# A fused attention and feed-forward layer: who applies the norms, in which order the first loads, roots and splits go, and the first projections in passes

## The chip, the cores and the metric

One core of one Trainium2 chip. The metric is the device time of one execution in microseconds; lower is better. The engines are PE (TensorE), DVE (VectorE), ACT (ScalarE), POOL (GpSimd) and SP (SyncE, which issues every DMA of this kernel).

## The reference

Everything is float32. `x` is (4, 256, 256): four sequences of 256 tokens with 256 features.

```python
xn = _layernorm(x, axis=-1)
s = attn(xn, Wqkv, Wproj, bproj)      # 16 heads of 16; softmax over the 256 keys of each sequence
g = silu(ffn(xn))                      # gelu(xn @ proj1.T + b1) @ proj2.T + b2, hidden 1024
x = x + s * g
```

## The kernel before

To keep float32 accuracy in fast matmuls, each factor of a product is split into a high part in the fp32r type and the remainder, a low part, in the same type (names ending in h and l). A product is three products: high x high, low weight x high x, high weight x low x. The function `product` issues them as passes `(a, b)`, where a is 0 for the high and 1 for the low part of the left factor (the weights, in the projections), and b the same for the right factor, each over two chunks `kc` of the 256 features. It puts a wait ahead of the first instruction that needs a part.

One list, `build_order()`, holds all steps in PE's order. Each engine walks through the list and does its own share of each step, so the list sets the order on PE, ACT and DVE alike. POOL and SP have programs of their own. Engines meet at counting semaphores.

The head of the kernel, which the change is about:

- SP loads x by sequences of 256 tokens (256 KB each, `x_in[b]`), and the weights `wqkv` in three chunks c of 256 KB: c = 0 is the queries' weights, 1 the keys', 2 the values'. Then come w1 and w2 (1 MB each), biases and wp.
- Norm of sequence b: DVE takes the statistics (`norm_stats`, two tiles of 128 tokens) and mean, variance + eps (`norm_eps`); POOL takes the power -1/2 (`rsqrt`, `rstd`). The norm is applied in place in `xs`. For sequences 0 and 1 ACT does it as scale x + shift (L380), for which DVE first makes `shift` = -mean x rstd (L476). For sequences 2 and 3 DVE does it itself, (x - mean) x rstd (L492).
- The weights: ACT copies chunk c to `wqh` (L375, "split"), POOL subtracts and makes `wql` (L332). Likewise w1 (ACT L406, POOL L344) and w2.
- `("XT", b)`: PE transposes the normed sequence b (L657, four f32 transposes); ACT copies two chunks to `xTh` (L392), DVE makes `xTl` (L517).
- `("QA", i)`: PE multiplies weight block i (0 and 1 queries, 2 and 3 keys) with sequence 0, six matmuls of 256 columns. `("QK", 0, i)` does the same block with sequence 1 in the other half of the same bank; then ACT copies the 512 columns to `stage` (L400), DVE makes the low half of it (L528), and SP issues three DMAs that rearrange them by heads into `qs` and `ks` (L293). `("QK", 1, i)` is sequences 2 and 3. `("V", h, p)` are the values, `("F1", n)` the first layer of the feed-forward part.
- The first scores `("S", 0)` (L699) wait for the twelve DMAs of half 0 (`stacked[0]`).
- Before all this PE runs `WARM` = 6 matmuls of 128x256 f32 on zeros (L635, each is two records), and one more, `KEEP` (L661), between XT 0 and QA 0.

The PSUM banks of later steps are given out in turn (`banks()`): V 0 takes the bank of QK (0, 0), so it waits until DVE has made its low half; V 1 takes that of QK (0, 1), QK (1, 0) that of QK (0, 2).

The order begins:

```python
order = [("XT", 0), ("KEEP",), ("QA", 0), ("QA", 1), ("XT", 1), ("QA", 2), ("QA", 3)]
order += [("QK", 0, i) for i in range(4)]
order += [("XT", 2), ("V", 0, 0), ("XT", 3), ("V", 0, 1)] + [("QK", 1, i) for i in range(4)]
order += [("F1", n) for n in range(FC)]
```

Of the kernel before, what the change touches and what calls it, by code (L numbers as in the profile page):

```python
# [5 lines left out]
B, SQ, E = 4, 256, 256  # L6
NH, HN = 16, 16
F = 1024
P = 128
# [8 lines left out]
GROUPS = B * 4  # L18
STK = 48
STM = STK + 2  # L20
WARM = 6
AHEAD = 6
VW = HN + 1
PAIRS = [(j, b) for half in range(2) for j in range(HP // 2) for b in (2 * half, 2 * half + 1)]
# [2 lines left out]
def build_order():  # L27

    order = [("XT", 0), ("KEEP",), ("QA", 0), ("QA", 1), ("XT", 1), ("QA", 2), ("QA", 3)]
    order += [("QK", 0, i) for i in range(4)]
    order += [("XT", 2), ("V", 0, 0), ("XT", 3), ("V", 0, 1)] + [("QK", 1, i) for i in range(4)]
    order += [("F1", n) for n in range(FC)]
    order += [("V", 1, p) for p in range(2)]

    ffn = [("F2", u, part) for u in range(TT) for part in range(4)]  # L40
    filler = [(s, 1) for s in ffn[:4 * TT // 2]] + [(("F1", n), 1.9) for n in range(FC, 2 * FC)]
    filler += [(s, 1) for s in ffn[4 * TT // 2:4 * TT // 2 + AHEAD]]
    ffn = ffn[4 * TT // 2 + AHEAD:]
    share = sum(w for _, w in filler) / len(PAIRS)
    at = 0
    for n in range(len(PAIRS)):
        while filler and at < (n + 1) * share - 0.5:
            step, w = filler.pop(0)
            order.append(step)
            at += w  # L50

        order += [("S", 2 * n), ("S", 2 * n + 1)]
        if n >= 2 and PAIRS[n - 2][1] == B - 1 and PAIRS[n - 2][0] < 2:
            order.append(("MT", PAIRS[n - 2][0]))
    assert not filler

    order.append(ffn.pop(0))
    for g in range(GROUPS):
        j, b = divmod(g, B)
        order += [("ST", 2 * g), ("ST", 2 * g + 1)]  # L60
        if g >= 1:
            order.append(("PV", g - 1))

        if g >= 1 and (j == 0 or b <= 1):
            order.append(ffn.pop(0))
        if g in (1, 2):
            order.append(("MT", g + 1))
        if g == GROUPS - 2:
            order.append(("GATE",))
        if b == 3:  # L70
            order.append(("TURN", 0, j))
        if b == 1 and j >= 1:
            order.append(("TURN", 1, j - 1))
        if b >= 2 and j >= 1:
            u = 2 * (j - 1) + b - 2
            if g < GROUPS - 1:
                order += [("PJ", u, 0), ("PJ", u, 1), ("FIN", u)]
            else:

                order += [("PJ", u, 0), ("PV", g), ("PJ", u, 1)]  # L80
    assert not ffn
    return order + [("PJ", 6, 0), ("PJ", 7, 0), ("TURN", 1, 3), ("FIN", 5), ("PJ", 6, 1), ("FIN", 6),
                    ("PJ", 7, 1), ("FIN", 7)]


def layer_kernel(nc, x, wqkv, w1, b1, w2, b2, wp, bp, out):
    f32, f32r = mybir.dt.float32, mybir.dt.float32r
    ALU, ACT, AX = mybir.AluOpType, mybir.ActivationFunctionType, mybir.AxisListType
    order = build_order()
# [5 lines left out]
    with ctx:  # L95
        def sem(name):
            return ctx.enter_context(nc.semaphore(name))
# [7 lines left out]
        def at(name, shape, dtype, where=None):  # L105
            size = 4
            for n in shape[1:]:
                size *= n
            if where is None:
                where = used[0]  # L110
                used[0] += (size + 31) // 32 * 32
                assert used[0] <= slab * 4, (name, used[0])
            return nc.alloc_sbuf_tensor_at(name, shape, dtype, offset=base + where)
# [53 lines left out]
        veps = at("veps", [P, TT], f32)  # L167
        mhalf = at("mhalf", [P, TT], f32)
        rstd = at("rstd", [P, TT], f32)
        shift = at("shift", [P, 4], f32)  # L170
        negm = at("negm", [P, HP // 2, 2, 2, 2, B], f32)
        mm = at("mm", [2 * HP * 2, 2, 2, P], f32r)
        rc = at("rc", [P, 2, SQ // 32], f32)
# [13 lines left out]
            sem(n) for n in ("wqkv_hi", "wqkv_lo", "w1_hi", "w1_lo", "w2_hi", "w2_lo"))  # L187
        stats_done, mv_done, veps_done, rstd_done, xn_done = (
            sem(n) for n in ("stats_done", "mv_done", "veps_done", "rstd_done", "xn_done"))
        shift_done = sem("shift_done")  # L190
        xt_made, xt_hi, xt_lo = sem("xt_made"), sem("xt_hi"), sem("xt_lo")
        qk_made, qk_hi, qk_lo = sem("qk_made"), sem("qk_hi"), sem("qk_lo")
        v_made, v_out, f1_made, gelu_done = sem("v_made"), sem("v_out"), sem("f1_made"), sem("gelu_done")
# [65 lines left out]
        def _(sp):  # L259
# [2 lines left out]
            out_t = out.rearrange("(b p t) e -> p b t e", p=P, t=2)  # L262
            for b in range(2):
                sp.dma_start(xs[:, 2 * b:2 * b + 2, :], x_t[:, b, :]).then_inc(x_in[b], 16)
            for c in range(2):
                sp.dma_start(wqkv_raw[:, c], wqkv[c]).then_inc(wqkv_in[c], 16)
            for b in range(2, B):
                sp.dma_start(xs[:, 2 * b:2 * b + 2, :], x_t[:, b, :]).then_inc(x_in[b], 16)
            sp.dma_start(wqkv_raw[:, 2], wqkv[2]).then_inc(wqkv_in[2], 16)
# [45 lines left out]
        def _(pool):  # L315
# [8 lines left out]
            def rsqrt(b):  # L324
                pool.wait_ge(veps_done, b + 1)
                nc.gpsimd.tensor_tensor(rstd[:, 2 * b:2 * b + 2], veps[:, 2 * b:2 * b + 2],
                                        mhalf[:, 2 * b:2 * b + 2], ALU.pow).then_inc(rstd_done, 1)

            pool.wait_ge(mhalf_set, 1)
            def low_wqkv(c):  # L330
                pool.wait_ge(wqkv_hi, c + 1)
                nc.gpsimd.tensor_tensor(wql[:, c], wqkv_raw[:, c], wqh[:, c].bitcast(f32),  # L332
                                        ALU.subtract).then_inc(wqkv_lo, 1)

            rsqrt(0)
            low_wqkv(0)
            rsqrt(1)
            low_wqkv(1)
            rsqrt(2)
            rsqrt(3)  # L340
            low_wqkv(2)
            for kc in range(KC):
                pool.wait_ge(w1_hi, kc + 1)
                nc.gpsimd.tensor_tensor(w1l[:, kc, :], w1_raw[:, kc, :], w1h[:, kc, :].bitcast(f32),  # L344
# [24 lines left out]
        def _(act):  # L369
# [4 lines left out]
                act.wait_ge(wqkv_in[c], 16)  # L374
                nc.scalar.activation(wqh[:, c], wqkv_raw[:, c], ACT.Copy).then_inc(wqkv_hi, 1)  # L375

            def norm_apply(b):
                act.wait_ge(shift_done, b + 1)
                for t in (2 * b, 2 * b + 1):
                    nc.scalar.activation(xs[:, t, :], xs[:, t, :], ACT.Identity, scale=rstd[:, t:t + 1],  # L380
                                         bias=shift[:, t:t + 1]).then_inc(xn_done, 1)

            split_wqkv(0)
            norm_apply(0)
            split_wqkv(1)
            n_qk = n_v = n_f1 = n_mt = 0
            for s in order:
                if s[0] == "XT":
                    b = s[1]
                    act.wait_ge(xt_made, b + 1)  # L390
                    for kc in range(KC):
                        nc.scalar.activation(xTh[:, kc, b * SQ:(b + 1) * SQ], bank[:, home[("XT", b)][kc], 0:SQ],  # L392
                                             ACT.Copy).then_inc(xt_hi, 1)
                    if b == 0:
                        norm_apply(1)
                        split_wqkv(2)
                elif s[0] == "QK":
                    h, i = s[1:]
                    act.wait_ge(qk_made, n_qk + 1)
# [66 lines left out]
        def _(dve):  # L466
# [3 lines left out]
                for t in (2 * b, 2 * b + 1):  # L470
                    nc.vector.bn_stats(stats[:, t, :], xs[:, t, :]).then_inc(stats_done, 1)

            def norm_shift(b):

                dve.wait_ge(rstd_done, b + 1)
                nc.vector.scalar_tensor_tensor(shift[:, 2 * b:2 * b + 2], mv[:, 2 * b:2 * b + 2, 0], -1.0,  # L476
                                               rstd[:, 2 * b:2 * b + 2], ALU.mult, ALU.mult).then_inc(shift_done, 1)

            def norm_eps(b):

                for t in (2 * b, 2 * b + 1):
# [20 lines left out]
            nc.vector.memset(warm[:], 0.0).then_inc(warm_set, 1)  # L502
            norm_stats(0)
            norm_eps(0)
            norm_stats(1)
            norm_shift(0)
            norm_eps(1)
            norm_stats(2)
            norm_shift(1)
            n_qk = n_mt = 0  # L510
            for s in order:
                if s[0] == "XT":
                    b = s[1]
                    cols = slice(b * SQ, (b + 1) * SQ)
                    for kc in range(KC):
                        dve.wait_ge(xt_hi, KC * b + kc + 1)
                        nc.vector.tensor_tensor(xTl[:, kc, cols], bank[:, home[("XT", b)][kc], 0:SQ],  # L517
                                                xTh[:, kc, cols].bitcast(f32), ALU.subtract).then_inc(xt_lo, 1)
                    if b == 0:
                        norm_eps(2)  # L520
                        norm_stats(3)
                    if b == 1:
                        norm_eps(3)
                        norm_apply(2)
                elif s[0] == "QK":
                    h, i = s[1:]
                    dve.wait_ge(qk_hi, n_qk + 1)
# [81 lines left out]
        def _(pe):  # L609
            def product(dst, lhs, rhs, chunks, first=True, last=True, rhs_hi=None, lhs_lo=None, rhs_lo=None,  # L610
                        passes=((0, 0), (1, 0), (0, 1))):

                todo = [(kc, a, b) for a, b in passes for kc in chunks]
                for n, (kc, a, b) in enumerate(todo):
                    if rhs_hi and (a, b) == (0, 0):
                        pe.wait_ge(rhs_hi[0], rhs_hi[1] + n + 1)
                    if rhs_lo and (a, b) == (0, 1):  # L620
                        pe.wait_ge(rhs_lo[0], rhs_lo[1] + n - 2 * len(chunks) + 1)
                    if lhs_lo and (a, b, kc) == (1, 0, chunks[0]):
                        pe.wait_ge(*lhs_lo)
                    m = nc.tensor.matmul(dst, lhs(kc, a), rhs(kc, b), start=first and n == 0,  # L624
                                         stop=last and n == len(todo) - 1)
                return m
# [7 lines left out]
                for _ in range(WARM):  # L634
                    nc.tensor.matmul(bank[:, 7, 0:HALF // 2], warm[:, 0:P], warm[:], start=True, stop=True)  # L635

            def project(s, at, width):

                i = s[2]
                cols = slice(at, at + width)  # L640
                seen = KC * (cols.stop // SQ - 1)
                return product(bank_of(*s)[:, at % HALF:at % HALF + width],
                               lambda kc, a: (wqh, wql)[a][:, i // 2, kc, (i % 2) * P:(i % 2 + 1) * P],
                               lambda kc, a: (xTh, xTl)[a][:, kc, cols], range(KC),
                               rhs_hi=(xt_hi, seen), lhs_lo=(wqkv_lo, i // 2 + 1), rhs_lo=(xt_lo, seen))

            pe.wait_ge(warm_set, 1)
            warm_up()
# [1 line left out]
            for s in order:  # L650
# [10 lines left out]
                    nc.tensor.matmul(bank[:, 7, 0:P], warm[:, 0:P], warm[:, 0:P], start=True, stop=True)  # L661
                elif s[0] == "QA":
                    pe.wait_ge(wqkv_hi, s[1] // 2 + 1)
                    project(("QK", 0, s[1]), 0, SQ)
                elif s[0] == "QK":
                    h, i = s[1:]
                    pe.wait_ge(wqkv_hi, i // 2 + 1)
# [133 lines left out]
```

## Time and profile before

| | us |
|---|---|
| median of 3 runs | 134.61 |
| lowest and highest | 133.0, 134.88 |
| the profiled execution, its own time | 134.43 |
| its span in the trace | 132.6 |

The span is what the trace covers, from the first to the last instruction of that execution; the 1.8 us beside it are start and end, outside the trace. All rows below are of this one execution. PEclk is the share of TensorE's full speed that was granted, 1.00 for 2.4 GHz and 0.50 for 1.2 GHz. In a timeline an xN row joins N instructions that follow one another; its second number is from the start of the first to the end of the last, so that instructions 0.12 us apart and 0.28 long show as x2 with 0.40.

### The profile page before, as it was taken

The page shows a single profiled execution, that of the slowest core. Times are in us where ns is not written, and L with a number is a line of the kernel's source. Part 1 is how long each engine was busy: PE and PEld are TensorE (multiplying, and loading weights), DVE is VectorE, ACT ScalarE, POOL GpSimd, SP SyncE. Part 2 cuts the span into 40 slices and gives each one's busy share as a digit, 9 for nine tenths or more (in the row PEclk, how much of TensorE's full clock was granted, in tenths as well). Part 3 has the DMA queues.
Part 4 walks back from the last instruction along what each step waited for, and adds up shares of the span by engine and source line. Part 5 has one row for each costly group of instructions (what it writes and reads, how often), then busy time and mean ns, then how long its engine had stood idle before and what let it go on. Part 6 is the DMA issues. An engine that isn't in the chain of part 4 may idle for free.

```text
span 132.6 us, 2665 instructions
## 1 busy us (share of the span) xinstructions
PE 123.1 (93%) x1002; PEld 94.8 (72%) x1002; DVE 88.0 (66%) x176; ACT 77.2 (58%) x119; POOL 51.2 (39%) x53
## 2 busy tenths in 40 slices
PE   6959999999999999999998999699999999999960
PEld 5639999888899989887676697466665666576550
DVE  0664584440001999999996899566768666858983
ACT  4264497489992101117658505769869787987610
POOL 3292468039999100005656560069604000004400
PEclk9995999999999999999999999999999999999995
DMA  4999459999999999940000000800000110110103
GB/s 134 325 400 395 115 121 146 159 164 141 166 167 147 168 169 147 168 66 7 0 0 0 2 12 10 302 14 10 15 0 5 40 42 5 40 42 2 42 2 119
DMA packets 7553, 13.29 MB, mean 100 GB/s; under 512 B 1012, under 2 KB 2676, under 8 KB 7284
## 3 DMA queue, kind: packets, MB, share of 16 engines
q1 hardware_dynamic: 7540, 13.11, 46.8%
q8 instruction: 8, 0.13, 0.5%
q14 instruction: 5, 0.04, 0.1%
HBM read 5.51 MB, written 1.05 MB: 49 GB/s over the span
## 4 chain that ended last, share of the span: by engine, by line
PE 74%; DVE 8%; ACT 6%; issue 4%; DMA 3%; POOL 1%; SPq 1%; ACTq 0%; DVEq 0%
PE bank L624 49%; PE bank L747 11%; PE bank L719 7%; PE bank L699 6%; DMA wqkv_raw<-wqkv 3%; ACT PT L450 3%; DVE negm L540 3%; PE bank L657 1%; DVE cd L557 1%; ACT hG L432 1%; POOL wql L332 1%; ACT cTh L462 1%; DVE shift L476 1%; DVE yh L582 1%; DVE fin L599 1%
## 5 line engine op out<-in xcount | busy, mean ns | idle before, releaser
L540 DVE TENSOR_REDUCE negm<-bank 128x4 f32<-128x1024 f32 x32 | 37.1, 1218 | 16.1 <-PE bank L699 16.0
L450 ACT ACTIVATE PT<-bank 128x1024 f32<-128x1024 f32 x32 | 30.7, 1020 | 6.4 <-PE bank L719 6.3
L353 POOL TENSOR_TENSOR hTl<-hG,hTh 128x512 fp32r<-128x512 f32 x16 | 20.4, 1293 | 23.3 <-ACT hTh L436 23.3
L363 POOL TENSOR_TENSOR bg<-gate,bps 128x256 f32<-128x256 f32 x8 | 6.1, 765 | 33.8 <-DVE gate L499 24.8
L747 PE MATMUL bank<-PT,VA 128*17 128x256 f32 x256 | 16.9, 382 | 0.0
L456 ACT ACTIVATE th<-yh 128x256 f32<-128x256 f32 x8 | 3.3, 418 | 21.4 <-DVE yh L582 21.4
L624 PE MATMUL bank<-w2h,hTh 128*128 128x256 f32 x64 | 14.7, 311 | 0.5 <-DVE yh L582 0.3
L719 PE MATMUL bank<-qs,ks 50*128 50x256 f32 x128 | 12.9, 310 | 1.4 <-ACT PT L450 1.4
L557 DVE STREAM_TRANSPOSE cd<-bank 128x256 f32<-128x256 f32 x16 | 7.2, 449 | 10.3 <-PE bank L747 10.3
L432 ACT ACTIVATE hG<-bank,b1s 128x512 f32<-128x512 f32 x16 | 10.9, 679 | 5.1 <-PE bank L624 5.1
L624 PEld LDWEIGHTS bank<-w2h,hTh 128*128 128x128 f32 x64 | 9.7, 189 | 5.5 <-issue 4.6
L624 PE MATMUL bank<-w2h,hTl 128*128 128x256 f32 x64 | 12.8, 282 | 0.0
L624 PE MATMUL bank<-w2l,hTh 128*128 128x256 f32 x64 | 12.8, 282 | 0.0
L719 PEld LDWEIGHTS bank<-qs,ks 50*128 50x128 f32 x128 | 8.8, 185 | 4.5 <-ACT PT L450 2.2
L699 PE MATMUL bank<-ks,qs 48*128 48x256 f32 x128 | 11.8, 303 | 0.0
L699 PEld LDWEIGHTS bank<-ks,qs 48*128 48x128 f32 x128 | 8.5, 185 | 3.5 <-issue 1.8
L624 PE MATMUL bank<-xTh,w1h 128*128 128x512 f32 x32 | 10.5, 410 | 0.4 <-ACT hG L432 0.4
L436 ACT ACTIVATE hTh<-hG 128x512 fp32r<-128x512 f32 x16 | 10.1, 633 | 0.5
L624 PEld LDWEIGHTS bank<-w2l,hTh 128*128 128x128 f32 x64 | 9.9, 191 | 0.0
L624 PE MATMUL bank<-xTh,w1l 128*128 128x512 f32 x32 | 9.9, 390 | 0.0
L624 PE MATMUL bank<-xTl,w1h 128*128 128x512 f32 x32 | 9.9, 390 | 0.0
L624 PEld LDWEIGHTS bank<-w2h,hTl 128*128 128x128 f32 x64 | 9.9, 190 | 0.0
(76 smaller groups left out, 212.0 us busy)
## 6 DMA issues: line engine op xcount, KB each, us to landing
qs<-stage SPq DMA_DIRECT2D x12, 256.0 KB, 13.1
ks<-stage SPq DMA_DIRECT2D x12, 256.0 KB, 18.7
w_raw<-w SPq DMA_DIRECT2D x2, 1024.0 KB, 8.2
xs<-x SPq DMA_DIRECT2D x4, 256.0 KB, 3.8
xb<-x SPq DMA_DIRECT2D x1, 1024.0 KB, 5.4
out<-fin SPq DMA_DIRECT2D x8, 128.0 KB, 1.7
wqkv_raw<-wqkv SPq DMA_DIRECT2D x3, 256.0 KB, 4.5
wps<-wp SPq DMA_DIRECT2D x8, 32.0 KB, 6.5
```

Of the source, the lines that this page charges most:

```text
L353: nc.gpsimd.tensor_tensor(hTl[:, n % FC, :], hG[:, n % FC, :], hTh[:, n % FC, :].bitcast(f32), ALU.subtract).then_inc(h_lo, 1)
L363: nc.gpsimd.tensor_tensor(bg[:, u % 2, :], gate[:, u, :], bps[:], ALU.mult).then_inc(bg_done, 1)
L432: nc.scalar.activation(hG[:, f, :], bank_of(*s), ACT.Gelu, bias=b1s[:, f:f + 1]).then_inc(gelu_done, 1)
L436: nc.scalar.activation(hTh[:, f, :], hG[:, f, :], ACT.Copy).then_inc(h_hi, 1)
L450: nc.scalar.activation(PT[:, w % 4], scores_of(*s), ACT.Exp).then_inc(exp_done, 1)
L456: nc.scalar.activation(th[:, u % 2, :], yh[:, u % 2, :], ACT.Tanh).then_inc(th_done, 1)
L540: nc.vector.tensor_reduce(negm[:, j, :, :, s[1] % 2, b].rearrange("p q a -> p a q"), scores_of(*s), axis=AX.X, op=ALU.max, negate=True).th ...
L557: nc.vector.transpose(cd[:, g % 2, :], bank_of(*s)[:, 0:SQ]).then_inc(cd_out, 1)
L624: m = nc.tensor.matmul(dst, lhs(kc, a), rhs(kc, b), start=first and n == 0, stop=last and n == len(todo) - 1)
L699: last = nc.tensor.matmul(scores_of(*s)[:, par, qt, :], qs[rows, hp, c:c + P], ks[rows, hp, b * SQ:(b + 1) * SQ], start=True, stop=True)
L719: last = nc.tensor.matmul(scores_of(*s)[:, par, kt, :], ks[rows, hp, c:c + P], qs[rows, hp, b * SQ:(b + 1) * SQ], start=True, stop=True)
L747: last = nc.tensor.matmul(bank_of(*s)[32 * m:32 * m + VW, 0:SQ], VA[:, 2 * b + kt, 4 * j + m, :], PT[:, w % 4, m % 2, kt, :], start=(kt == ...
```

## The change

1. SP loads x 0, weights 0, x 1, weights 1, x 2, x 3, weights 2, in place of x 0, x 1, weights 0, weights 1, x 2, x 3, weights 2.
2. DVE applies the norm of all four sequences. `shift` is gone, and ACT applies none.
3. DVE's order: stats 0, eps 0, apply 0, stats 1, eps 1; after the low part of XT b, for b = 0 and 1: apply b+1, stats b+2, eps b+2. Apply 3 stays behind the low half of the first QK.
4. ACT splits weight chunk 1 behind its copies of XT 0 and chunk 2 behind those of XT 1.
5. POOL's root of sequence c goes ahead of the low part of weight chunk c for c = 0, 1, 2, and the root of sequence 3 goes behind the low part of chunk 2 (before, it went ahead of it).
6. The projections of sequence 0 go in passes: for the query blocks 0 and 1 high x high of both, low weights of both, low x of both; for the key blocks high x high and low x of both, then XT 1, then the low weights of both. XT 1 moves behind these passes. The waits in `product` count by chunk.
7. `WARM` is 4 in place of 6.

```diff
-WARM = 6
+WARM = 4
...
-    order = [("XT", 0), ("KEEP",), ("QA", 0), ("QA", 1), ("XT", 1), ("QA", 2), ("QA", 3)]
+    order = [("XT", 0), ("KEEP",)]
+    order += [("QA", i, a, b) for a, b in ((0, 0), (1, 0), (0, 1)) for i in (0, 1)]
+    order += [("QA", i, a, b) for a, b in ((0, 0), (0, 1)) for i in (2, 3)]
+    order += [("XT", 1)] + [("QA", i, 1, 0) for i in (2, 3)]
...
             for b in range(2):
                 sp.dma_start(xs[:, 2 * b:2 * b + 2, :], x_t[:, b, :]).then_inc(x_in[b], 16)
-            for c in range(2):
-                sp.dma_start(wqkv_raw[:, c], wqkv[c]).then_inc(wqkv_in[c], 16)
+                sp.dma_start(wqkv_raw[:, b], wqkv[b]).then_inc(wqkv_in[b], 16)
...
-            def low_wqkv(c):
+            for c in range(3):
+                rsqrt(c)
                 pool.wait_ge(wqkv_hi, c + 1)
                 nc.gpsimd.tensor_tensor(wql[:, c], wqkv_raw[:, c], wqh[:, c].bitcast(f32),
                                         ALU.subtract).then_inc(wqkv_lo, 1)
-
-            rsqrt(0)
-            low_wqkv(0)
-            rsqrt(1)
-            low_wqkv(1)
-            rsqrt(2)
             rsqrt(3)
-            low_wqkv(2)
...
             split_wqkv(0)
-            norm_apply(0)
-            split_wqkv(1)
...
-                    if b == 0:
-                        norm_apply(1)
-                        split_wqkv(2)
+                    if b <= 1:
+                        split_wqkv(b + 1)
...
             norm_stats(0)
             norm_eps(0)
+            norm_apply(0)
             norm_stats(1)
-            norm_shift(0)
             norm_eps(1)
-            norm_stats(2)
-            norm_shift(1)
...
-                    if b == 0:
-                        norm_eps(2)
-                        norm_stats(3)
-                    if b == 1:
-                        norm_eps(3)
-                        norm_apply(2)
+                    if b <= 1:
+                        norm_apply(b + 1)
+                        norm_stats(b + 2)
+                        norm_eps(b + 2)
...
-                        pe.wait_ge(rhs_hi[0], rhs_hi[1] + n + 1)
+                        pe.wait_ge(rhs_hi[0], rhs_hi[1] + kc + 1)
...
-                        pe.wait_ge(rhs_lo[0], rhs_lo[1] + n - 2 * len(chunks) + 1)
+                        pe.wait_ge(rhs_lo[0], rhs_lo[1] + kc + 1)
...
-                    project(("QK", 0, s[1]), 0, SQ)
+                    end = (1, 0) if s[1] >= 2 else (0, 1)
+                    project(("QK", 0, s[1]), 0, SQ, passes=(s[2:],), first=s[2:] == (0, 0), last=s[2:] == end)
```

## Rows read from the trace of the kernel before

**Rows 1.** The page, busy time of PE: us (share of the span) and instructions.
```profile
PE 123.1 (93%) x1002; PEld 94.8 (72%) x1002; DVE 88.0 (66%) x176; ACT 77.2 (58%) x119; POOL 51.2 (39%) x53
```

**Rows 2.** The chain of waits in order of time: start us, us, what.
```profile
1.65 4.28 DMA wqkv_raw<-wqkv
...
5.95 0.64 ACT wqh L375
...
10.22 2.19 PE bank L624 x8
...
13.27 4.53 PE bank L624 x36
```

**Rows 3.** Stretches: PE, PEld, DVE, ACT, POOL busy (instructions), PEclk, DMA share, GB/s.
```profile
6.70:10.20 3.50, 1.86 (x10) 1.27 (x10) 2.34 (x5) 2.37 (x6) 3.12 (x3) 1.00 1.02 407
10.20:13.60 3.40, 3.38 (x15) 3.34 (x16) 1.27 (x6) 1.57 (x5) 0.69 (x1) 0.50 1.01 390
13.70:70.00 56.30, 56.30 (x383) 48.46 (x383) 36.36 (x51) 29.80 (x51) 27.53 (x19) 1.00 0.78 118
```

**Rows 4.** Timeline: start us, us, engine, line, what, count [idle before <-releaser].
```profile
1.19 5.49 PE L635 MATMUL bank<-warm 128*128 128x256 f32 x12 [1.19 <-DVE warm L502]
...
3.45 0.75 DVE L471 BATCH_NORM_STATS2 stats<-xs 128x6 f32<-128x256 f32 x2 [2.32 <-DMA xs<-x]
...
4.78 0.71 POOL L326 TENSOR_TENSOR rstd<-veps,mhalf 128x2 f32<-128x2 f32 x1 [2.76 <-DVE veps L485]
...
6.48 1.08 ACT L380 ACTIVATE xs<-xs,shift,rstd 128x256 f32<-128x256 f32 x2
...
7.21 0.84 PE L657 MATMUL bank<-ident,xs 128*128 128x128 f32 x4 [0.54 <-ACT xs L380]
...
8.08 0.66 ACT L392 ACTIVATE xTh<-bank 128x256 fp32r<-128x256 f32 x2
...
8.54 1.28 POOL L332 TENSOR_TENSOR wql<-wqkv_raw,wqh 128x512 fp32r<-128x512 f32 x1
...
8.61 0.57 PE L624 MATMUL bank<-xTh,wqh 128*128 128x256 f32 x2 [0.34 <-ACT xTh L392]
8.61 1.22 DVE L476 SCALAR_TENSOR_TENSOR shift<-mv,rstd 128x2 f32<-128x2 f32 x1 [0.58 <-POOL rstd L326]
...
10.22 0.92 PE L624 MATMUL bank<-xTl,wqh 128*128 128x256 f32 x2 [0.81 <-DVE xTl L517]
...
12.21 1.05 PE L657 MATMUL bank<-ident,xs 128*128 128x128 f32 x4
...
13.30 0.66 ACT L392 ACTIVATE xTh<-bank 128x256 fp32r<-128x256 f32 x2 [1.83 <-PE bank L657]
...
15.67 1.32 ACT L400 ACTIVATE stage<-bank 128x512 fp32r<-128x512 f32 x2 [1.71 <-PE bank L624]
...
16.30 0.69 DVE L528 SCALAR_TENSOR_TENSOR stage<-bank,stage 128x512 fp32r<-128x512 f32 x1 [0.83 <-ACT stage L400]
...
17.09 3.91 SPq L293 DMA_DIRECT2D qs<-stage  x6
...
17.64 0.60 PE L657 MATMUL bank<-ident,xs 128*128 128x128 f32 x4
...
42.12 0.74 PE L699 MATMUL bank<-ks,qs 48*128 48x256 f32 x8
```

**Rows 5.** Single lines of the code: duration ns min/median/max, first and last start us.
```profile
L380 ACT ACTIVATE xs<-xs,shift,rstd x4: 585/585/600, 6.5 to 10.4; 128x256 f32<-128x256 f32 x4
L492 DVE TENSOR_SCALAR xs<-xs,mv,rstd x4: 404/408/409, 14.7 to 17.2; 128x256 f32<-128x256 f32 x4
L536 DVE TENSOR_SCALAR b2s<-b2s x1: 284/284/284, 28.3 to 28.3; 128x256 f32<-128x256 f32 x1
```

**Rows 6.** Landing of the second DMA (x 1), and of ks copies issued 23.0 to 25.0.
```profile
DMA to landing us min/median/max: 2.8/2.8/2.8
...
DMA to landing us min/median/max: 12.2/14.0/15.1
```

More of the change, by code:

```diff
@@ L169, in layer_kernel @@
         rstd = at("rstd", [P, TT], f32)
-        shift = at("shift", [P, 4], f32)
         negm = at("negm", [P, HP // 2, 2, 2, 2, B], f32)
@@ L189, in layer_kernel @@
             sem(n) for n in ("stats_done", "mv_done", "veps_done", "rstd_done", "xn_done"))
-        shift_done = sem("shift_done")
         xt_made, xt_hi, xt_lo = sem("xt_made"), sem("xt_hi"), sem("xt_lo")
@@ L375, in split_wqkv @@
                 nc.scalar.activation(wqh[:, c], wqkv_raw[:, c], ACT.Copy).then_inc(wqkv_hi, 1)
[L377 to L381, printed above, removed]
             split_wqkv(0)
-            norm_apply(0)
-            split_wqkv(1)
             n_qk = n_v = n_f1 = n_mt = 0
@@ L471, in norm_stats @@
                     nc.vector.bn_stats(stats[:, t, :], xs[:, t, :]).then_inc(stats_done, 1)
[L473 to L477, printed above, removed]
             def norm_eps(b):
@@ L635, in warm_up, with project @@
                     nc.tensor.matmul(bank[:, 7, 0:HALF // 2], warm[:, 0:P], warm[:], start=True, stop=True)
-            def project(s, at, width):
+            def project(s, at, width, **passes):
                 i = s[2]
@@ L644, in project @@
                                lambda kc, a: (xTh, xTl)[a][:, kc, cols], range(KC),
-                               rhs_hi=(xt_hi, seen), lhs_lo=(wqkv_lo, i // 2 + 1), rhs_lo=(xt_lo, seen))
+                               rhs_hi=(xt_hi, seen), lhs_lo=(wqkv_lo, i // 2 + 1), rhs_lo=(xt_lo, seen), **passes)
             pe.wait_ge(warm_set, 1)
```

## The prediction

> **What bounds the kernel now.** I read first the busy shares and the granted clock of the page: PE is busy 93% of the span [rows 1], and no other engine above 66%. An edit to the head is worth time only if the matmuls behind it start earlier, so I went to the chain of waits [rows 2]. The reader is to see in it two parts. Up to 10.2 us it hops between engines: the load of the first weights, their split on ACT, then their low part and a root on POOL, a norm's shift on DVE, the low half of x. From 10.22 us it is PE without a break, of which two pieces stand in the rows. From 13.7 to 70 us PE is busy for all of 56.30 us [rows 3], and the other engines are started by its products there. So what the change is worth is by how much the dense stretch gets ahead. I measure this at one place: the start of the transposes of sequence 2, XT 2, now 17.64 [rows 4]. Behind it PE issues the same instructions in the same order in both kernels.
>
> Then the clock. The head has a low stretch: 0.50 granted from 10.2 to 13.6, 1.00 before and after [rows 3]. Prices differ by it. Four f32 transposes of 128 columns took 1.05 us inside (12.21) and 0.60 outside (17.64) [rows 4]; less the length of the last, 0.42 and 0.27, they are 0.21 and 0.11 apart. Projections of 256 f32r columns: 36 in 4.53 us, 0.12 to 0.13 each, nearly all outside [rows 2]; inside I take 0.21, half that speed. The 12 warm-up records took 5.49 us, 0.43 apart, for 256 f32 columns [rows 4]; from 0.11 for 128 such columns they would be 0.22 apart at the high level. So the warm-up ran at 1.2 GHz, although the clock reads 1.00 there: the rows show no level before the first switch, and by the projections at 8.61 (two in 0.57 us, against 0.92 for two at 10.22) 2.4 GHz had been reached.
>
> **Part by part.** *Norm 0 on DVE.* Now: rstd of POOL at 4.78 + 0.71 = 5.49; shift on DVE; the two applies on ACT only from 6.48, 0.59 long [rows 5], since they are queued behind the split of the weights, whose load lands at 1.65 + 4.28 = 5.93 [rows 2, 4]. XT 0 starts at 7.21. After: DVE applies from 5.53, two 0.33 us apart, as the two statistics of the same size at 3.45 (0.75 less 0.41) [rows 4], and 0.41 long [rows 5], done at 5.94 and 6.26. ACT's two norms (1.08 us the pair) and two shifts go away. XT 0, which starts 0.14 us behind the first apply (7.21 against 6.48 + 0.59), starts at 6.08. At the low level XT 1 shows 13.30 - 12.21 = 1.09 from the first transpose to the first copy on ACT [rows 4], so xTh(0) is copied from 7.17 and the first projection starts 0.53 behind (8.61 - 8.08), at 7.70 instead of 8.61. Gain here: 0.9.
>
> *Loads by turns.* The first weights move from third to second place, x of sequence 1 from second to third. The second place, issued at 1.2, landed 2.8 later at 4.0, and the third at 5.93 [rows 2, 6]. If place decides, the split is done long before 7.2; if the tensor decides, it is as now, 5.95 + 0.64 = 6.59, which also is in time, and POOL's low part is done at 7.9, in time for the second pass. x 1 at 5.93 is wanted by DVE at 6.27, behind the applies. So: nothing, and 0.3 us if x 1 came 0.7 late. The later loads keep their places.
>
> *WARM 6 to 4, and the passes.* Four warm-ups end at 1.19 + 8 x 0.43 = 4.6; none of this lies on the path, and its only price is the clock. Passes let four high matmuls run while the low weights and the low half of x are made, where now PE waits 0.81 us for xTl(0) at 10.22 with all blocks behind it [rows 4]. At the low level the 12 matmuls of the two query blocks take 12 x 0.213 = 2.56, to 10.26. The low half of x: from the start of stats 0 to that of the root went 4.78 - 3.45 = 1.33 us [rows 4], so DVE does stats 1 and eps 1 from 6.27 to 7.5, then xTl(0) (twice 0.37) to 8.25; its pass comes at 9.4, so no wait.
>
> *Norm 1.* POOL's root follows eps 1: 7.6 to 8.3; the apply follows xTl(0) on DVE: 8.34 to 9.1. Now this shift of two elements a partition takes 1.22 us [rows 4], from the start of POOL's wql(1) at 8.54 to its end at 9.82: DVE stood for POOL. The apply reads one tensor where the shift read two, and I cost it at its own 0.41. XT 1 now waits for the norms, and xTh(1) until 13.30. After: with the high level from 10.26, eight matmuls of the key blocks 10.26 to 11.25, XT 1 to 11.7, the four low-weight ones to 12.2 (POOL's low 1 is done by 9.6), xTh(1) from 11.95, QK 0 from 12.45, 24 matmuls of 0.12 = 2.9: XT 2 at 15.35. **Gain 17.64 - 15.35 = 2.3 us.**
>
> *What is late next.* DVE gets new work: the queue behind xTl(1) (12.35 to 13.05) is apply 2, stats 3, eps 3 (to 14.95), then the low half of QK 0 (0.69 [rows 4]) to 15.6, apply 3 to 16.4, QK 1 to 17.05. Waiting for these: V 0 for the first bank and POOL's wql(2) (14.5), at 15.8, just covered; XT 3 at 17.25 for apply 3, covered by 0.8; V 1 for the second bank at 17.7, covered. On POOL rstd 3 now stands behind wql(2), 1.28 us: 15.0 to 15.7, which is the time above. On ACT the splits of chunks 1 and 2 move behind the xTh copies of sequences 0 and 1, but stage 0 starts at 13.25 against 15.67 [rows 4], 2.4 earlier, so ACT's queue keeps up with PE. SP waits for the low half: its first copy of the stage leaves at 15.7 instead of 17.09, only 1.4 earlier, while PE is 2.3 earlier. The last of the 12 copies that the first S needs is issued at 25.0 and lands 15.1 later, at 40.1 [rows 6]; S starts at 42.12 [rows 4]. Slack falls from 2.0 to 1.1. It stays covered; if the copies shifted not at all, 0.3 would be lost.
>
> All of 2.3 us should arrive at the end: 134.43 - 2.3 = **132.1 us** (span 130.3). The profiled run lies 0.18 below the median, so the reference is good for either; of three runs one was at 133.0.
>
> **The rule that speaks against it.** The apply with pointer scalars takes 404 to 409 ns, a scaling by a constant of the same shape 284 [rows 5]: the apply does not run in whatever form makes the other fast. The Trainium skill (SBUF — State Buffer, Who interferes with whom) says that tensor_scalar can enter a mode that takes the pair of ports that DVE shares with GpSimd, and that the second of the two to start is then held for the whole instruction of the first. By this rule the applies would stand as the shift did; the duration speaks against it, and no row here has an apply beside a long POOL instruction.
>
> **Rivals.**
> (a) *The clock rises earlier*, before 8.6 as it did in this run, in spite of the shorter warm-up. Then the projections run at 0.12, bounded by xTl(0) at 8.25, xn(1) at 9.1 and wql(1) at 9.6: XT 1 at 9.9, QK 0 at 11.0, XT 2 at 13.9. 3.7 earlier: 130.7. For it: nothing else is in the way. Against it: PE is idle between 4.6 and 6.1 and has small work until 7.7, and with as small work from 6.7 to 10.2 (1.86 of 3.50 us busy) the level fell [rows 3].
> (b) *The clock stays low longer*, until 13.7: of the 3.4 us after 10.26 half is lost, 1.7; gain 0.6: 133.8. My 10.26 is a choice: the one low stretch shown was 3.4 us long with matmuls throughout, and I laid the same length behind the start of steady work, which is between 7.0 (XT 0's end) and 7.7, so 10.3 to 11.1. Gaps in the passes, for xTh(0), wqh(1) or the norm of sequence 1, could put the rise off.
> (c) *DVE stands for POOL after all.* Apply 3 and POOL's first w1l (twice the size of wql, so 2 x 1.28 = 2.6 us) become ready together at 15.7. If they exclude each other and POOL is first, apply 3 ends at 19.0 instead of 16.4 and XT 3 waits 1.75 us: gain 0.55, 133.9. The shift at 8.61 shows such a wait [rows 4]. Against it the duration above.
> (d) *Slower: the clock never settles in the head.* The mechanism is the cut of the warm-up from 5.5 to 3.4 us ahead of an idle 1.5; each 3.4 us at low inside dense work costs 1.7. If it also stayed low from 13.7 to 17.1, this is another 1.7: 135.5. It decides from where the low level lasts past 14.9 (gain used up: 2.3 = half of 4.6).
>
> **How the numbers follow.** Main case (rise near 10.3, the queues cover) 55%, 131.5 to 132.9: DVE's and ACT's queues are within 0.3 us of binding at two places, and an earlier or later rise by 1 us gives 0.5 either way. (a) 18%, (b) 12%, (c) 6%, (d) 4%; the last 5% something unseen, both ways. The prediction is 132.1. The range reaches from (a) to beyond (b) and (c): 130.6 to 134.1. About 2% is what a measurement here tells from no change; that border is 131.9, inside the main case, just under its middle. Faster by over 2%: all of (a), two in five of the main case and a bit: 0.43. Same: 0.52. Slower: 0.05.
>
> **What would show it.** First transposes near 6.1, first projection near 7.7; XT 1 near 11.2; XT 2 near 15.3 and PE without idle from there to the first S near 39.8; the shift's 1.22 us gone and all eight applies at 0.41; first stage copy issued near 15.7. PE's granted clock is the number to look at first: if the rise isn't at 10 to 11, (a), (b) or (d) holds, and the time follows by half of what is left at low. Wrong otherwise: a wait of V 0 for the low half of QK 0, of XT 3 for apply 3, or of S for the copies.

## The result and the profile after

The changed kernel is slower: 139.8 us median of 4 runs (139.22 to 140.82) against 134.75 of 4 (133.0 to 137.3); ratio 1.047, 95% interval 1.040 to 1.054. I had forecast 132.1, range 130.6 to 134.1. The profiled execution took 140.17 us, its span is 138.3 (before: 132.6).

Executions of one and the same kernel spread by 1 to 6% here (before: 133.0 to 137.3), so ratios below are of those within 1.5% of their kernel's fastest.

The page after, PE and granted clock in 40 slices of 3.46 us:

```profile
PE   6489955999999999999999899969999999999970
...
PEclk9968996589999999999999999999999999999999
```

PE has a hole in the sixth and seventh slice (17 to 24 us) that was not there, and the clock two dips (0.50 from 8.1 to 11.5 us and from 21.7 to 28.5), of which the second was not there. The timeline after, in the form of [rows 4]:

```profile
4.17 0.63 ACT L371 ACTIVATE wqh<-wqkv_raw 128x512 fp32r<-128x512 f32 x1 [1.94 <-DMA wqkv_raw<-wqkv]
...
5.60 1.26 POOL L335 TENSOR_TENSOR wql<-wqkv_raw,wqh 128x512 fp32r<-128x512 f32 x1
5.68 1.66 DVE L473 TENSOR_SCALAR xs<-xs,mv,rstd 128x256 f32<-128x256 f32 x2 [0.90 <-POOL rstd L328]
...
7.16 0.67 PE L634 MATMUL bank<-ident,xs 128*128 128x128 f32 x4 [2.29 <-DVE xs L473]
...
9.16 1.28 POOL L335 TENSOR_TENSOR wql<-wqkv_raw,wqh 128x512 fp32r<-128x512 f32 x1
9.23 1.68 DVE L473 TENSOR_SCALAR xs<-xs,mv,rstd 128x256 f32<-128x256 f32 x2 [0.15 <-POOL rstd L328]
...
16.48 0.60 PE L634 MATMUL bank<-ident,xs 128*128 128x128 f32 x4
...
16.65 0.68 DVE L505 SCALAR_TENSOR_TENSOR stage<-bank,stage 128x512 fp32r<-128x512 f32 x1
...
17.43 7.43 SPq L295 DMA_DIRECT2D qs<-stage  x6
17.48 4.73 POOL L340 TENSOR_TENSOR w1l<-w_raw,w1h 128x1024 fp32r<-128x1024 f32 x2
17.48 0.47 PE L601 MATMUL bank<-wqh,xTh 128*128 128x256 f32 x2 [0.41 <-DVE stage L505]
17.55 4.81 DVE L473 TENSOR_SCALAR xs<-xs,mv,rstd 128x256 f32<-128x256 f32 x2 [0.21 <-POOL rstd L328]
...
20.16 0.41 PE L634 MATMUL bank<-ident,xs 128*128 128x128 f32 x2 [1.02 <-DVE xs L473]
...
22.41 0.69 PE L634 MATMUL bank<-ident,xs 128*128 128x128 f32 x2 [1.85 <-DVE xs L473]
```

Look at DVE's applies (L473) and at the POOL row beside each. In the kernel before, a pair of applies took 0.73 us (0.41 each, 0.33 apart):

```profile
14.74 0.73 DVE L492 TENSOR_SCALAR xs<-xs,mv,rstd 128x256 f32<-128x256 f32 x2
```

Here it takes 1.66 and 1.68 beside a wql and 4.81 beside both w1l. The last pair of the change taken apart, DVE and POOL:

```profile
17.48 2.38 POOL L340 TENSOR_TENSOR w1l<-w_raw,w1h 128x1024 fp32r<-128x1024 f32 x1
17.55 2.46 DVE L473 TENSOR_SCALAR xs<-xs,mv,rstd 128x256 f32<-128x256 f32 x1 [0.21 <-POOL rstd L328]
...
19.82 2.38 POOL L340 TENSOR_TENSOR w1l<-w_raw,w1h 128x1024 fp32r<-128x1024 f32 x1
...
19.93 2.43 DVE L473 TENSOR_SCALAR xs<-xs,mv,rstd 128x256 f32<-128x256 f32 x1
```

Each apply ends 0.15 us behind the end of a POOL subtraction, and the second meets the second subtraction. XT 3 waits for both tiles: 1.02 + 1.85 us of idle PE. Then the clock, in stretches as in [rows 3]:

```profile
8.50:11.70 3.20, 3.20 (x16) 3.20 (x17) 3.05 (x8) 0.55 (x2) 1.93 (x2) 0.54 1.01 421
21.90:25.20 3.30, 2.78 (x12) 2.41 (x13) 3.30 (x8) 0.66 (x2) 0.31 (x1) 0.50 0.75 127
25.40:28.40 3.00, 3.00 (x10) 2.42 (x10) 0.08 (x1) 0.61 (x1) 0.00 (x0) 0.50 1.09 138
29.00:75.00 46.00, 46.00 (x307) 38.57 (x306) 29.15 (x33) 22.88 (x38) 19.96 (x15) 1.00 0.80 104
```

PE was nearly idle from 19.1 to 22.4 (busy 0.45 us), and the clock is at 1.2 GHz (0.50 granted) from 21.7 to 28.5. PE is busy for 6.1 us of that, so by my estimate half of this is lost, some 3.0 us.

Where the time came, by five places of PE's program (us from the start of the trace). The first three kernels are before, after, and the experiment e2, in which POOL stays out of the applies' way; e7 and e12 are the change taken apart:

| | XT 0 | XT 2 | QK (1, 0) | first S | span |
|---|---|---|---|---|---|
| before | 7.21 | 17.64 | 21.38 | 42.12 | 132.6 |
| after | 7.16 | 16.48 | 25.81 | 47.86 | 138.3 |
| e2 | 5.87 | 15.20 | 19.00 | 39.91 | 130.9 |
| e7, loads, passes, WARM alone | 7.85 | 17.16 | 20.90 | 41.69 | 132.5 |
| e12, norms, splits, roots alone | 6.16 | 15.38 | 23.53 | 45.57 | 136.5 |

Up to XT 2 the change gains 1.16 us. Between XT 2 and QK (1, 0) it loses 9.33 - 3.74 = 5.6: 0.41 for QK 0's low half, 2.9 for the applies, and 2.3 more, of which the slow clock is some 1.7 (3.4 us busy at 0.50) and the rest isn't told apart. From there to the first S another 1.3 go to the slow clock. The end is 5.7 late, as the first S is.

### The profile page after: what moved, and what is told of

Read it like the earlier page. It is cut to its first block, busy times and chain, and to the rows that moved or that the text cites. A ratio compares the mean times of both kernels' runs of the same rounds, so it can differ in the third digit from the quotient of the medians.

```text
span 138.3 us, 2663 instructions
## 1 busy us (share of the span) xinstructions
PE 124.5 (90%) x998; PEld 95.6 (69%) x998; DVE 94.8 (69%) x178; ACT 75.3 (54%) x115; POOL 51.0 (37%) x53
## 4 chain that ended last, share of the span: by engine, by line
PE 70%; DVE 15%; ACT 6%; issue 4%; DMA 2%; POOL 1%; ACTq 0%; DVEq 0%; POOLq 0%
PE bank L601 46%; PE bank L725 10%; PE bank L697 6%; PE bank L677 6%; DVE xs L473 6%; ACT PT L437 3%; DVE negm L517 3%; DMA xs<-x 2%; PE bank L634 1%; POOL rstd L328 1%; DVE stats L458 1%; DVE cd L534 1%; ACT hG L419 1%; ACT cTh L449 1%; DVE yh L559 1%
## 5 line engine op out<-in xcount | busy, mean ns | idle before, releaser
L473 DVE TENSOR_SCALAR xs<-xs,mv,rstd 128x256 f32<-128x256 f32 x8 | 9.9, 1272 | 1.3 <-POOL rstd L328 1.3
```

The costliest lines, as they stand in the source:

```text
L473: nc.vector.tensor_scalar(xs[:, t, :], xs[:, t, :], mv[:, t, 0:1], rstd[:, t:t + 1], ALU.subtract, ALU.mult).then_inc(xn_done, 1)
```

## The experiments

**e1: w1l behind apply 3.**

```diff
                 pool.wait_ge(w1_hi, kc + 1)
+                pool.wait_ge(xn_done, TT)
```

> POOL's two w1l subtractions wait until DVE has applied norm 3. Exclusion theory (an apply and a POOL subtraction can't run together; apply 3 waited for both w1l and that is the loss): apply 3 falls from 4.81 us to 0.73, XT 3 starts near 19.0 instead of 22.4, no second low stretch of the clock at 21.9, QK (1, 0) near 20.9 against 21.3 before: about 134.0 us, level with before or 0.5 below. Rival (the order of the passes, the serial queue on DVE or the shorter warm-up are the loss): stays at 138 or more.

Four runs took 134.21 to 138.63 us (before in the same set: 133.53 to 137.51). The traced one took 136.3, with this head: apply 3 took 0.73 us, XT 3 began at 19.14, there was no second low stretch at 22 (the next is at 86.9 to 90.3), QK (1, 0) came at 21.01. The exclusion theory holds for the largest piece. What I hadn't expected: the first S waited.

```profile
17.70 0.73 DVE L474 TENSOR_SCALAR xs<-xs,mv,rstd 128x256 f32<-128x256 f32 x2 [0.21 <-POOL rstd L328]
...
42.59 0.74 PE L678 MATMUL bank<-ks,qs 48*128 48x256 f32 x8 [0.76 <-DMA ks<-stage]
```

**e2: all of POOL's lows behind the applies.** As e1, and for each weight chunk

```diff
                 rsqrt(c)
                 pool.wait_ge(wqkv_hi, c + 1)
+                pool.wait_ge(xn_done, 2 * (c + 1))
```

> Besides w1l, each wql(c) on POOL waits until DVE has applied norm c. Exclusion theory: all eight applies take 0.41, XT 0 starts near 6.2 instead of 7.2, XT 2 near 15.5 instead of 16.5, QK (1, 0) near 19.2 to 19.6: 132.2 to 133.0 us, what my prediction had. Rival (POOL's later lows become the wait: V 0 for wql(2)): 134 or more.

Four runs took 132.55, 132.68, 135.05 and 136.75 us. The timeline of the one of 132.68:

```profile
5.31 0.73 DVE L475 TENSOR_SCALAR xs<-xs,mv,rstd 128x256 f32<-128x256 f32 x2 [0.91 <-POOL rstd L328]
5.87 1.09 PE L636 MATMUL bank<-ident,xs 128*128 128x128 f32 x4 [0.90 <-DVE xs L475]
...
15.20 0.60 PE L636 MATMUL bank<-ident,xs 128*128 128x128 f32 x4
...
15.57 4.62 SPq L295 DMA_DIRECT2D qs<-stage  x6
...
39.91 0.74 PE L679 MATMUL bank<-ks,qs 48*128 48x256 f32 x8
```

All pairs are back at 0.73 us, and the head is the one that I had forecast for the change itself (XT 2 at 15.35, first copy at 15.7, first S at 39.8). One hold is left, on the small eps step (0.17 us alone), which meets wql(2):

```profile
13.56 1.30 POOL L336 TENSOR_TENSOR wql<-wqkv_raw,wqh 128x512 fp32r<-128x512 f32 x1 [2.32 <-DVE xs L475]
...
14.33 0.55 DVE L468 TENSOR_SCALAR veps<-mv 128x2 f32<-128x2 f32 x1
```

It stands ahead of the low half of QK 0 in DVE's queue, so SP's first copy could leave some 0.4 us earlier still, by estimate.

**e3: the applies in a form that also accumulates.** POOL is as in the change. The accumulating form uses its second operation to reduce, so the norm's scaling is left out here.

```diff
                     nc.vector.tensor_scalar(xs[:, t, :], xs[:, t, :], mv[:, t, 0:1], rstd[:, t:t + 1],
-                                            ALU.subtract, ALU.mult).then_inc(xn_done, 1)
+                                            ALU.subtract, ALU.mult,
+                                            accum_out=spare[:, t:t + 1]).then_inc(xn_done, 1)
```

> The applies also write an accumulator that nobody reads; POOL is left as in the changed kernel. If it is the two-port form of the apply that excludes POOL, and this form has none, the applies take about 0.54 us each (twice 0.13 for 256 elements more) beside POOL's work and the time is 132.5 to 133.5. If the two pointer scalars are what is read through the shared port, the applies still wait for POOL and the time stays at 139 to 140.

Half right. The applies wait for nobody, with w1l beside them:

```profile
14.69 0.54 DVE L474 TENSOR_SCALAR_CACHE_REDUCE xs<-xs,mv,rstd 128x256 f32<-128x256 f32 x1 [0.21 <-POOL rstd L329]
14.69 4.76 POOL L341 TENSOR_TENSOR w1l<-w_raw,w1h 128x1024 fp32r<-128x1024 f32 x2
...
41.85 0.74 PE L679 MATMUL bank<-ks,qs 48*128 48x256 f32 x8 [2.94 <-DMA ks<-stage]
```

It still reads both pointer scalars, so these are not what collides. But the time is 136.57 (ratio 1.017, 1.006 to 1.029), although QK (1, 0) is at 18.05, 3.3 us ahead of before. The first S waits 2.94 us for the last copy of half 0, and the clock is at 0.50 from 42.8 to 46.2 and again from 87.1 to 90.5. The head can be made faster than the copies behind it.

**e4: WARM = 6** in the changed kernel.

> Changed kernel with WARM = 6. Exclusion theory: apply 3 still takes 4.8 us, the time stays within 0.8 us of 139.8. Clock theory (the two warm-ups that were cut are the loss): the low stretch at 8.5 to 11.7 moves or goes and the time falls by 2 us or more.

138.79 us, ratio to before 1.033 (1.022 to 1.044): 1.0 below the changed kernel in medians, more than I gave it. Apply 3 still took 4.81. In its trace there is no low stretch in the first 21 us, XT 2 is at 15.10, and the one behind the hole lasts 3.4 us where the changed kernel's lasted 6.8; there is one more, from 90.0 to 93.4. So the warm-up may be worth a microsecond here, by where the clock's switches fall; one trace of each can't settle that. It is not the loss.

**e5: SP holds its copies of half 1.** As e2, and

```diff
             for h in range(2):
+                if h == 1:
+                    sp.wait_ge(stacked[0], 192)
```

> As e2, and SP holds its copies of half 1 until the twelve of half 0 have landed. In e1 and in the accumulator run the first S waited 0.8 and 2.9 us for the last copy of half 0, which had been on its way 17.4 us, where before it was 15.1. If the copies of half 1, which now come early, slow those of half 0, the last ks copy of half 0 lands 1 us or more earlier than in e2 and no wait is left ahead of the first S; time as e2 or up to 1 us less. If the copies don't disturb one another, nothing changes. If holding them is too much, the first S of the second half (near 61) waits and the time is above e2.

The theory that the halves disturb each other isn't borne out. From the first issue to the first S: 24.7 us here, with nothing of half 1 in the queue, 24.3 in e2, and 25.8 in e13, the same kernel as e2. With such a spread between two traces of one kernel, an effect of a microsecond could hide. What the hold did was to make the second half late, by 3.67 us, with the clock at 0.50 from 62.5 to 69.3. Four runs took 136.46 to 140.37 us.

```profile
38.94 0.74 PE L681 MATMUL bank<-ks,qs 48*128 48x256 f32 x8 [0.39 <-DMA ks<-stage]
...
63.74 1.23 PE L681 MATMUL bank<-ks,qs 48*128 48x256 f32 x8 [3.67 <-DMA ks<-stage]
```

**e7: the kernel before with the loads, the passes and WARM = 4 alone.** (The diff of the change, its parts 1, 6 and 7.)

> The kernel before with the order of loads, the passes of the projections and WARM = 4 alone; norms 0 and 1 stay on ACT, POOL keeps its order. If the norms on DVE are the whole loss and the passes are worth what PE waited at 10.2 (0.8 us), this runs 0.5 to 1 us below before, XT 2 near 17. Rival (the passes or the short warm-up lose by themselves, by putting XT 1 later and by a longer low stretch): 135 to 137 us, XT 2 at 18 or later.

Neither: ratio 1.003 (0.998 to 1.007), no difference; the median of the ten runs is 134.7 us, against 134.53 of before. XT 2 came at 17.16, 0.5 earlier, in spite of an XT 0 that was 0.6 later:

```profile
6.93 0.14 DVE L478 SCALAR_TENSOR_TENSOR shift<-mv,rstd 128x2 f32<-128x2 f32 x1
7.11 1.09 ACT L382 ACTIVATE xs<-xs,shift,rstd 128x256 f32<-128x256 f32 x2 [2.27 <-DVE shift L478]
```

The shift stood behind stats 1 on DVE, and x 1 was now the third load. Passes and loads are worth something, about 0.5 us at QK (1, 0), and don't lose by themselves. Here too apply 3, which was on DVE before the change already, met wql(2): its pair took 1.25 us, covered.

**e12: norms, splits and roots alone**: the changed kernel with the loads, the order of projections and WARM of before.

> Changed kernel with the loads, the order of the projections and WARM = 6 of before: only the norms on DVE, the splits' places and POOL's order stay. Exclusion theory: apply 3 still meets w1l and the pairs of 0 to 2 meet wql, so the loss is all here: 138.5 to 140.5 us, and with the passes alone at 134.7 the two parts add up to the whole. Rival (it takes both parts for the loss): under 137.

138.82 us, ratio 1.035 (1.026 to 1.044); apply 3 again 4.81 us beside w1l, a low stretch from 22.9 to 26.3. With e7's 0.3% this is most of the 4.7%; 1 us is left.

The two parts are not independent, though. With the weights third again, wql(0) begins at 6.95 us, behind apply 0, which is free:

```profile
5.60 0.74 DVE L471 TENSOR_SCALAR xs<-xs,mv,rstd 128x256 f32<-128x256 f32 x2 [0.91 <-POOL rstd L326]
...
6.95 1.27 POOL L333 TENSOR_TENSOR wql<-wqkv_raw,wqh 128x512 fp32r<-128x512 f32 x1 [1.39 <-ACT wqh L369]
```

In the change the weights land second, wql(0) begins at 5.60 and holds the pair to 1.66 us, and XT 0 is 1.0 later (7.16 against 6.16). So the earlier weights, harmless in e7, took away the gain of norm 0. Whether this is the 1 us that is left isn't shown: e4, with the early weights but WARM = 6 as in e12, also took 138.8 us. e12 and e4 have in common that no low stretch is recorded before 21 us (XT 2 at 15.38 and 15.10), where the change has one from 8.1 to 11.5.

**e8 and e9: what form the apply has.** e8 puts constants in place of the pointers, so the norm is left out; e9 cuts each apply in two.

```diff
# e8
-                    nc.vector.tensor_scalar(xs[:, t, :], xs[:, t, :], mv[:, t, 0:1], rstd[:, t:t + 1],
+                    nc.vector.tensor_scalar(xs[:, t, :], xs[:, t, :], 0.0, 1.0,
# e9
+                    for part in range(2):
+                        half = slice(part * P, (part + 1) * P)
+                        last = nc.vector.tensor_scalar(xs[:, t, half], xs[:, t, half], mv[:, t, 0:1],
```

> Changed kernel whose applies take the constants 0.0 and 1.0 in place of mean and rstd, so the norm is left out. If the two-port form is what excludes POOL, these also wait for w1l (4.8 us for the last pair), and one alone takes 0.28 us as L536 did. If the pointer scalars are what collides, they take 0.28 us everywhere and never wait.

> Each apply of 256 columns is made as two of 128. It shows which form the apply with pointer scalars has when alone: at one column a cycle (0.13 us for 128) a half takes 0.27 us; at two, 0.34 us, and then the 0.12 us over the form with constants are a fixed cost of the pointers and say nothing of the form. My prediction took the 0.40 against 0.28 for the slow form.

The first pair of e8, its last pair, and the first of e9 (duration ns min/median/max):

```profile
L473 DVE TENSOR_SCALAR xs<-xs x2: 280/812/1345, 5.5 to 6.7; 128x256 f32<-128x256 f32 x2
...
17.29 4.81 DVE L473 TENSOR_SCALAR xs<-xs 128x256 f32<-128x256 f32 x2 [0.21 <-POOL rstd L328]
```

```profile
L475 DVE TENSOR_SCALAR xs<-xs,mv,rstd x4: 334/334/1274, 5.5 to 7.2; 128x128 f32<-128x128 f32 x4
```

Their one run each took 140.16 and 142.22 us. With constants an apply alone takes 0.28 us and waits for w1l just the same. With pointers and half the columns it takes 334 ns against 404: 70 ns for 128 columns. The accumulating form of e3 took 0.54 for 256, 0.14 more than the plain one; if that is the price of going one column at a time, 256 cost 0.28 in it and 0.14 in the plain form, again 0.07 for 128, with 0.26 fixed in both. So, by this estimate, the apply runs in a form twice as fast per column as that of e3. Its 0.40 against 0.28 is then a fixed cost of the pointers, if the form with constants has the same rate; that form was timed at 256 columns only. The Trainium skill (VectorE: DVE Perf Modes, Mode 2×_2P — use both read ports for one tensor) says that an fp32 tensor_scalar gets two results a cycle by streaming halves of one tensor through both ports; these rows agree.

**e10: POOL writes and doesn't read.** w1's low part is left out: `memset(w1l)` in place of the subtraction.

> Changed kernel in which POOL's two w1l subtractions are memsets of w1l, so w1's low part is left out; POOL then writes SBUF but reads nothing. If the apply only collides in reading, apply 3 takes 0.73 us for the pair beside the memsets. If it also collides in writing, it waits for each memset.

```profile
17.12 0.95 POOL L340 MEMSET w1l<- 128x1024 f32 x1
17.21 1.32 DVE L472 TENSOR_SCALAR xs<-xs,mv,rstd 128x256 f32<-128x256 f32 x2 [0.21 <-POOL rstd L328]
18.41 1.02 POOL L340 MEMSET w1l<- 128x1024 f32 x1 [0.34 <-ACT w1h L392]
```

The pair takes 1.32 us, 0.6 more: it stands for the first memset, which writes only. 135.05 us in its one run.

**e13 and e14: e2 again, and e2 with WARM = 6**, in five rounds.

> The version in which POOL's low parts stay behind the applies, again, for an interval: 132.5 to 133.5 us, 1 to 2% under before. It can't be much less: the last copy of half 0 lands some 24.5 us behind the first issue, so the first S starts at 39.9.

> The same with WARM = 6. If the shorter warm-up costs through the clock, this is 0.3 to 1 us faster than the one with 4; the first S is then held by the copies at 39 to 40 in both and the difference stays under 0.5. If the warm-up is worth nothing, no difference.

e13: ratio 0.994 (0.988 to 1.001), no gain that can be told from nothing. e14: 0.980 (0.972 to 0.988), but from the two lowest of twelve runs (131.41, 131.66); the median of all twelve is 136.13 against 135.34 of before, so I don't call it faster. Their profiled executions took 135.44 and 138.23 us. In both, the first S stood and waited for the copies, 1.48 and 2.31 us:

```profile
40.35 0.74 PE L679 MATMUL bank<-ks,qs 48*128 48x256 f32 x8 [1.48 <-DMA ks<-stage]
```

```profile
41.75 1.22 PE L679 MATMUL bank<-ks,qs 48*128 48x256 f32 x8 [2.31 <-DMA ks<-stage]
```

But the wait is the smaller part of what e13 lost. It is the same kernel as e2, and its first S is only 0.44 us behind that of e2; at 83 us it is still 0.44 behind. Then the clock goes to 1.2 GHz from 83.7 to 90.6, and the last matmul is 2.8 us behind:

```profile
84.20:90.80 6.60, 6.60 (x51) 3.59 (x51) 2.25 (x6) 3.76 (x6) 5.36 (x8) 0.52 0.04 12
```

In e2, PE had the same two idle pieces just before (0.65 and 0.42 us), and the clock stayed at 1.00. Such a stretch of 3.4 us stands near 90 in the traces of e1, e3, e4, e5 and e14 too, and in none of the others; e14 has another from 41.4 to 48.2. What decides in which execution the clock falls there, no run shows. Much of the spread of the runs may be this: it is far from the head and as large as the gain that I had forecast. No version here beats the kernel before in all its runs.

## Why the prediction was wrong

**The step that failed** is the cost of the moved norms: "The apply reads one tensor where the shift read two, and I cost it at its own 0.41". It was costed as free of POOL because "the duration speaks against it". Measured, a pair, forecast at 0.73 us, took 1.66 to 1.70 us beside a wql and 4.81 beside both w1l. The inference took 404 ns against 284 for a slower form; e9 shows only 70 ns per 128 columns, so most of the 404 is fixed. The duration of one size can't tell the form. I also read the shift's 1.22 us rightly as DVE standing for POOL, and then took its reason (two tensors read) for the only one. The Trainium skill's rule (SBUF — State Buffer, Who interferes with whom) was the better guide, and rows after agree with it: the apply that starts second is held for the whole instruction of POOL, 2.46 us beside 2.38. That POOL's writing is enough is e10's (1.32 us for the pair).

**Rival (c) was the case**, at 6% and at 133.9. Its mechanism and place were right. Its price was short in three ways: not one w1l but one for each of the two applies (4.81 us, where I had 2.6 + 0.73); POOL's wql also held the pairs of norms 0, 1 and 2, 0.95 us each, so that XT 0 didn't gain at all; and an idle PE was costed at its own length, although the clock then falls (6.1 us of work at half speed, 3.0 lost).

**What held, and what was luck.** With POOL out of the way (e2) the working comes out place by place in the execution traced: XT 0 at 5.87 (I had 6.08), XT 2 at 15.20 (15.35), first stage copy at 15.57 (15.7), first S at 39.91 (39.8), 132.68 us (132.1). The choice that the clock is low through the first projections was right there: the row reads 1.00, as it does ahead of the first recorded switch, but four of them took 1.20 us from 7.52, and XT 1 at 10.96 was at full speed (four transposes in 0.60). Part of this match is luck. In e13, the same kernel, XT 0 at 6.16 was at full speed already (0.67 us for four), XT 2 came at 14.31, nearer to rival (a)'s 13.9 than to 15.35, and the first S only at 40.35, since it stood. And in e2 the last copy of half 0 landed at 39.9 us, so the copies had caught up with the head there. The gain of 2.3 us isn't shown even without the collisions: e13's ratio, 0.994, is under 1% and can't be told from none. "What is late next" named V 0's wait for QK 0's low half as "just covered": it was in e2, and in the change PE stood 0.41 us. "If place decides" was right for the loads: the first weights, now second, were split from 4.17.

**What was also too light**: "It stays covered" for the first S. The slack of 2.0 us was one execution's. The copies land 23.0 to 27.3 us behind the first issue over the kernels traced (before 23.0, e2 24.3, e5 24.7, e3 27.3), so the cover of 1.1 that I left was within their spread, and in e13 and e14 1.48 and 2.31 us were given back there. (d), slower by a clock that stays low, had the right ingredient with the wrong trigger: not the shorter warm-up, but a hole in PE's work at 19 us.

## What to carry to other kernels

Before a step moves to VectorE, list what GpSimd runs at that time; a tensor_scalar on tensors in SBUF stood here for the whole length of each GpSimd instruction that had started before it, so the short one must be put ahead of the long one with a wait, not left to race it. Moving a load can start such a race too, by making the GpSimd instruction ready earlier. A duration at one size doesn't tell which form an instruction runs in: take two sizes, or one beside a long neighbour. Price a hole in PE's work with the clock behind it, and a gain in PE's work with the next transfer it will have to wait for. And before a difference between two executions is put down to the place that was changed, follow it to the end of the trace: e13 lost most of its time 43 us behind the first S.

## What the runs showed of the hardware that I had not expected

- A tensor_scalar with pointer scalars took 0.12 us more than one with constants (0.40 against 0.28 for 256 columns), but only 70 ns for each 128 columns, by estimate half of what e3's form takes.
- GpSimd's memset, which reads nothing, held the apply as well (1.32 us for a pair in place of 0.73).
- The accumulating form (0.54 us) wasn't held, neither beside wql nor beside w1l (e3).
- Even a tensor_scalar of two elements a partition was held: 0.17 us alone, 0.55 (e2) and 1.00 (e12) beside a wql.
- A load's landing went by its place in the queue: the second landed 2.8 to 3.3 us behind its issue, whether it was x or weights, and the third 3.2 to 5.3.
- The same two idle pieces of PE near 83 us (0.65 and 0.42) were followed by a stretch at 1.2 GHz in one execution (e13) and by none in another of the same kernel (e2).
